# The diagonal term of a chunk's product, folded into the decay matrix by GpSimd

## The chip, the cores and the metric

The kernel runs on one core of a Trainium2 chip. The core has TensorE (matrix products, with its own queue of weight loads), VectorE, ScalarE and GpSimd (element by element), and SyncE, which here issues all DMAs. Each engine runs its own instructions in order and they wait for each other by semaphores. TensorE writes only to PSUM, and GpSimd reads only SBUF. The metric is the device time of one execution in microseconds, lower is better.

## The reference, cut to what matters

Four sequences of 512 tokens of width 256 go through a mixture of experts, a state space layer ("attention") and the mixture again. The change is in the state space layer. It has 64 heads with 128 state rows and 8 channels each, and does for each token t of each head:

```python
h  = at[..., None, None] * h + einsum('bh,bhn,bhp->bhnp', bt, B_prev, x_prev) \
                             + einsum('bh,bhn,bhp->bhnp', gt, Bt, xt)
yt = einsum('bhn,bhnp->bhp', Ct, h)
# alpha = exp(dt * A);  beta = (1 - lam) * dt * alpha;  gamma = lam * dt
```

So the state takes the token's own contribution with the weight gamma, and one step later the same contribution again with beta of the next step. All contributions of a token to later tokens have the weight `coef` = gamma + (1 - lam_next) * dt_next, times the decay; its contribution to its own output has gamma alone. That is the diagonal term.

## The kernel before, in words

An execution is two passes of three stages: the mixture for two sequences, the state space layer for each of the two, the mixture again. For the state space layer the 64 heads form 32 pairs, and the 512 tokens form 8 chunks of 64. A pair's work is spread over several turns of a software pipeline. Turn j (`turn_pe`, `turn_act`, `turn_pool`, `turn_dve`, `turn_sp`, one for each engine) treats pairs of different age side by side: projections for pair n+3 (`A`, matrix products at L61), angles for pair n+1 (`T`, L786 to L795), scaling and rotation of pair n (`F`), the chunk products of pair n-1 (`K`) and the output of pair n-2 (`Y`). Four turns (j = 0 to 3) form an iteration; one batch has 32 turns. The order within a turn is written out by hand for each engine, and nothing reorders it except that weight loads run ahead on TensorE.

The steps that matter here, in a turn:

- `F_dve1` (L885) multiplies the projections by the norm. `F_dve2` makes the decay matrix `dk` of pair n by a scan over the shift mask and the decay factors (L891), strictly below the diagonal, and a small masked copy `xwp` (L896). `F_dve3` (L909, four instructions of 128x1024) prepares the rotation, and `F_pool` (L917, L918, four of 128x512 on GpSimd) finishes it.
- `K1_pe` (L943) forms the products C·B of each chunk of pair n-1 into PSUM and transposes the rotated B (L951). `K_dve1` multiplies the products by the decay matrix into `m1` (L967) and by the diagonal mask into `m2` (L968), each in two halves of 128x256. `K2_pe` (L983) forms the chunks' states, `K_dve2` (L990, L994) runs the scan over the chunks.
- `Y1_pe` (L1005) multiplies `m1` by `x1p` and `m2` by `x2p`, 16 products of 64 tokens by 16 columns, each issued as two instructions. `x1` is x times `coef` and `x2` is x times gamma; both are made once for a batch in `prep_dve` (L720, L721), and `XP_act` (L930) puts each pair's part in place with four activations. `Y2_pe` (L1014) adds what comes from earlier chunks. Every fourth turn `Y_dve` (L1026, L1030) takes y out of PSUM.
- `ss_pe` (L827) sums squares for the norm; its second half waits for the first L846 of VectorE's turn. The second L846 of the turn waits for ScalarE's L840, which waits for the second projection (L61) of TensorE's turn.

VectorE's order in an ordinary turn is L786, L789, L846, L885 (two), L891, L896, L795, L846, L967/L968 (four), L856 in every second turn, L909 (two), L990, L994, L909 (two). TensorE's is `T` (L61), L1005, L61, L827, L1014, L61, L943 with L951, L61, L983, L61.

Of the kernel before, what the change touches and what calls it, by code (L numbers as in the profile page):

```python
# [14 lines left out]
P = 128  # L15
# [50 lines left out]
def build(nc, x_in, w_ffn, w_router, w_att, w_x, w_z, w_dtl, w_dth, a_log, w_out, bias_in, norm_w_in,  # L66
          sel_ffn_in, ident_in, cst_in, out):
    with ExitStack() as ctx:
# [67 lines left out]
        btr = sb("btr", [P, 2, SEQ])  # L136
        x1, x2 = sb("x1", [P, NH, TT, HP]), sb("x2", [P, NH, TT, HP])
        x1p = [sb(f"x1p{i}", [P, P]) for i in range(4)]
        x2p = [sb(f"x2p{i}", [P, P]) for i in range(4)]
        xwp = [sb(f"xwp{i}", [P, P]) for i in range(2)]  # L140
# [19 lines left out]
        dks = [xc[:, i, :] for i in range(2)]  # L160
        m1, m2 = sq[:, 0, :], sq[:, 1, :]
        one, cum = sb("one", [P, 1]), sb("cum", [P, SEQ])
# [498 lines left out]

        PREP_STEPS = 10
        e_pd, e_pu, e_p6 = ev("e_pd"), ev("e_pu"), ev("e_p6")
# [7 lines left out]
        def prep_dve(e, b):  # L671
# [41 lines left out]
            step(e.tensor_tensor(dlt, oml, dtk[:, 1], ALU.mult))  # L713
            step(e.tensor_tensor(coef, gam, dlt, ALU.add))
            assert n[0] == PREP_STEPS
            wide = lambda a, t: a[:, t, :].unsqueeze(2).to_broadcast([P, NH, HP])
            for t in range(TT):
                e.wait_ge(e_p2.sem, e_p2.at(TT * b + t + 1))
                src = xbanks[t][:, :].rearrange("p (n d) -> p n d", n=NH)
                e.tensor_tensor(x1[:, :, t, :], src, wide(coef, t), ALU.mult)  # L720
                ins = e.tensor_tensor(x2[:, :, t, :], src, wide(gam, t), ALU.mult)  # L721
            ins.then_inc(e_x12.sem, 1)
# [190 lines left out]
        def F_pool(e, n, j, types):  # L913
# [5 lines left out]
            if ty == 1:  # L919
                ins.then_inc(e_R.sem, 1)  # L920

        def XP_act(e, n, j, q):

            e.wait_ge(e_Y.sem, e_Y.at(n - 3))
            for dst, src in ((x1p, x1), (x2p, x2)):
                v = src[:, bass.ds(2 * q, 2) if not isinstance(q, int) else slice(2 * q, 2 * q + 2), :, :]
# [33 lines left out]
        def K_dve1(e, p, j):  # L960
            e.wait_ge(e_G.sem, e_G.at(p + 1))
            e.wait_ge(e_D.sem, e_D.at(p + 1))
            e.wait_ge(e_Y.sem, e_Y.at(p))
            half, dk = slice(0, SEQ // 2), dks[j % 2]
            for a in range(2):
                g, c = W[3 if a == 0 else 0][:, half], slice(a * SEQ // 2, (a + 1) * SEQ // 2)
                e.tensor_tensor(m1[:, c], g, dk[:, c], ALU.mult)  # L967
                ins = e.tensor_tensor(m2[:, c], g, constant("diag_mask")[:, c], ALU.mult)  # L968
            ins.then_inc(e_M.sem, 1)
# [26 lines left out]
        def Y1_pe(e, p, j, yev):  # L996
# [4 lines left out]
            for a in range(2):  # L1001
                for t in range(TT):
                    o = y[0:CL, 2 * t:2 * t + 2, PW * j + HP * a:PW * j + HP * a + HP]
                    for n, (m, x) in enumerate(((m1, x1p), (m2, x2p))):
                        e.matmul(o, m[:, (a * TT + t) * CL:(a * TT + t + 1) * CL], c4(x[j][:, :])[:, a * TT + t],  # L1005
                                 start=n == 0, stop=n == 1)

# [92 lines left out]
        def turn_pool(e, b, it, first, last):  # L1100

            N, Q, NB = b * NP + it * UN, it * UN, NP // UN
            for j in range(UN):
                n, q, p, jp = N + j, Q + j, N + j - 1, (j - 1) % UN
                T, A, SS, RG, K = in_turn(j, first, last)
                gm = b * (NP // 2) + it * 2 + j // 2
                F_pool(e, n, j, [0])
                F_pool(e, n, j, [1])
# [104 lines left out]
        def pairs_pool(e, b):  # L1213
            N, NB, G = b * NP, NP // UN, b * (NP // 2)
            turn_pool(e, b, 0, True, False)
            with e.Fori(1, NB - 1) as it:
# [269 lines left out]
```

## Time and profile before

| | us |
|---|---|
| median of 3 runs | 4703.65 |
| lowest and highest | 4689.84 and 4712.97 |
| the profiled execution | 4701.72 |
| its span | 4699.9 |
| TensorE busy in the span | 4481.7 (95%) |
| VectorE busy | 3160.8 (67%) |
| ScalarE busy | 2074.3 (44%) |
| GpSimd busy | 1383.5 (29%) |

The profile comes from one execution. In its rows PE is TensorE, PEld its weight loads, DVE VectorE, ACT ScalarE, POOL GpSimd and SP SyncE. PEclk is the granted clock of TensorE as a share of 2.4 GHz, a mean of moments at 2.4 and at 1.2 GHz. Matrix products overlap in the pipeline, so a single product's recorded time is longer than its share of the engine; the distance from one start to the next is the better measure. Busy shares are means over stages with different limits, so a stage has to be read for itself. The state space layer's pair loops lie at about 570 to 1170, 1245 to 1850, 2910 to 3510 and 3590 to 4195 us of the span.

### The profile page before, as it was taken

To read this page: it belongs to the slowest core of one execution; us is meant where nothing else is said; L and a number is where in the kernel's file an instruction comes from. 1 tells how busy PE (TensorE), PEld (TensorE's weight loads), DVE (VectorE), ACT (ScalarE), POOL (GpSimd) and SP (SyncE) were. 2 spreads that over 40 slices of the span, in tenths; PEclk is the share of its full clock that TensorE was granted. 3 is DMA by queue.
4 is the path that set the end of the run, shared out by engine and by line. 5 is a ranking of instruction groups with operands and counts; after the bars stand their busy time and mean duration, and the time that the engine had idled before them with its cause. 6 is when DMAs were issued, how large, how long until landed. Compare 5 with 4: busy or idle time off the path is not lost.

```text
span 4699.9 us, 89732 instructions
## 1 busy us (share of the span) xinstructions
PE 4481.7 (95%) x31616; PEld 3417.3 (73%) x31616; DVE 3160.8 (67%) x4157; ACT 2074.3 (44%) x3624; POOL 1383.5 (29%) x843
## 2 busy tenths in 40 slices
PE   8999899999799998999999997999988999999999
PEld 6777577877587786777667775877865787776776
DVE  5555499996599996444455554999955899954444
ACT  3333455552456552333233334555625565523332
POOL 3555133332133332111135551333321333311111
PEclk9999899997799997999999998999978999969999
DMA  4444444441444541111035544444414445411110
GB/s 151 175 175 165 155 137 147 137 142 43 131 136 141 148 128 42 57 41 41 23 142 184 186 165 140 140 148 140 134 41 134 141 134 150 124 41 47 49 44 20
DMA packets 231554, 542.73 MB, mean 115 GB/s; under 512 B 45112, under 2 KB 96320, under 8 KB 223168
## 3 DMA queue, kind: packets, MB, share of 16 engines
q1 hardware_dynamic: 231360, 540.26, 35.9%
q8 instruction: 108, 1.77, 0.2%
q14 instruction: 86, 0.70, 0.0%
HBM read 448.67 MB, written 90.44 MB: 115 GB/s over the span
## 4 chain that ended last, share of the span: by engine, by line
PE 76%; DVE 13%; issue 6%; DMA 2%; SPq 1%; ACT 1%; DVEq 1%; ACTq 0%
PE bank L61 47%; PE bank L943 4%; PE bank L983 4%; PE bank L1014 4%; PE bank L410 3%; PE bank L1005 3%; PE bank L827 3%; DVE rot L909 3%; PE bank L951 2%; DVE tmp L909 2%; DVE xbc L885 2%; DVE sqs L846 1%; PE bank L1255 1%; DVE bank L786 1%; DVE xc L891 1%
## 5 line engine op out<-in xcount | busy, mean ns | idle before, releaser
L917 POOL TENSOR_TENSOR rot<-rot,tmp 128x512 f32<-128x512 f32 x256 | 333.6, 1303 | 1918.5 <-DVE tmp L909 1918.5
L493 POOL TENSOR_TENSOR w_lo<-w_raw,w_hi 128x768 fp32r<-128x768 f32 x192 | 366.5, 1911 | 1336.5 <-ACT w_hi L453 1160.1
L61 PE MATMUL bank<-xh,wb 128*128 128x512 f32 x2048 | 704.8, 425 | 29.2 <-DVE sqs L846 26.3
L835 ACT ACTIVATE xbc<-bank,norm_w 128x512 f32<-128x512 f32 x512 | 350.3, 684 | 707.4 <-PE bank L61 699.6
L444 ACT ACTIVATE h_hi<-hf 128x512 fp32r<-128x512 f32 x384 | 242.8, 632 | 945.9 <-DVE hf L531 931.8
L526 DVE TENSOR_TENSOR h<-sg,bank 128x512 f32<-128x512 f32 x384 | 262.8, 684 | 548.1 <-PE bank L61 548.1
L61 PE MATMUL bank<-xh,w_hi 128*128 128x512 f32 x1536 | 603.7, 393 | 7.8 <-DVE xl L255 5.6
L61 PE MATMUL bank<-xl,w_hi 128*128 128x512 f32 x1536 | 600.8, 391 | 0.0
L61 PE MATMUL bank<-xh,w_lo 128*128 128x512 f32 x1536 | 597.2, 389 | 0.0
L533 DVE TENSOR_TENSOR h_lo<-hf,h_hi 128x512 fp32r<-128x512 f32 x384 | 379.0, 987 | 309.6 <-ACT h_hi L444 309.6
L61 PEld LDWEIGHTS bank<-xh,wb 128*128 128x128 f32 x2048 | 356.8, 193 | 104.8 <-DVE sqs L846 33.3
L918 POOL TENSOR_TENSOR rot<-rot,tmp 128x512 f32<-128x512 f32 x256 | 413.1, 1614 | 0.0
L909 DVE SCALAR_TENSOR_TENSOR tmp<-xbc,bias,cs_sn 128x1024 f32<-128x1024 f32 x256 | 411.9, 1609 | 0.0
L61 PE MATMUL bank<-xl,wb 128*128 128x512 f32 x1024 | 411.5, 402 | 0.0
L909 DVE SCALAR_TENSOR_TENSOR rot<-xbc,bias,cs_sn 128x1024 f32<-128x1024 f32 x256 | 359.7, 1405 | 1.5 <-PE bank L1014 1.4
L429 ACT ACTIVATE sg<-bank 128x512 f32<-128x512 f32 x384 | 229.9, 599 | 282.9 <-PE bank L61 282.0
L61 PE MATMUL bank<-h_hi,w_hi 128*128 128x512 f32 x784 | 351.8, 449 | 0.0
L61 PEld LDWEIGHTS bank<-xh,w_hi 128*128 128x128 f32 x1536 | 288.8, 188 | 69.4 <-issue 6.0
L61 PEld LDWEIGHTS bank<-xl,w_hi 128*128 128x128 f32 x1536 | 288.6, 188 | 64.9
L61 PEld LDWEIGHTS bank<-xh,w_lo 128*128 128x128 f32 x1536 | 288.7, 188 | 63.6
L885 DVE TENSOR_TENSOR xbc<-xbc,rr_bc 128x1024 f32<-128x1024 f32 x256 | 318.2, 1282 | 10.3 <-DMA rr_bc<-rr_dram 9.8
L61 PE MATMUL bank<-h_lo,w_hi 128*128 128x512 f32 x784 | 310.2, 396 | 0.0
(165 smaller groups left out, 8440.4 us busy)
## 6 DMA issues: line engine op xcount, KB each, us to landing
wb<-watt_dram SPq DMA_DIRECT2D x128, 1024.0 KB, 6.6
w_raw<-w_ffn SPq DMA_DIRECT2D x64, 1152.0 KB, 5.2
rr_bc<-rr_dram SPq DMA_DIRECT2D x128, 512.0 KB, 6.5
pw_raw<-w_att SPq DMA_DIRECT2D x64, 640.0 KB, 6.0
watt_dram<-pw_hi SPq DMA_DIRECT2D x64, 640.0 KB, 2.9
watt_dram<-pw_raw SPq DMA_DIRECT2D x64, 640.0 KB, 4.5
th<-watt_dram SPq DMA_DIRECT2D x128, 256.0 KB, 4.2
dt_bc<-row_dram SPq DMA_DIRECT2D x256, 128.0 KB, 3.1
```

The lines of the kernel that those rows point to most:

```text
L61: ins = e.matmul(dst, a, m, start=start and c == 0, stop=stop and c == n - 1, skip_group_check=not (start and stop))
L429: e.activation(sg[s][:, :], gate_bank[s][:, :], ACT.Silu).then_inc(e_silu.sem, 1)
L444: e.activation(h_hi[hslot(i, s)][:, :], hf[s][:, :], ACT.Copy).then_inc(e_hh.sem, 1)
L493: e.tensor_tensor(piece(w_lo[s], i), piece(w_raw[s], i), piece(w_hi[s], i).bitcast(F32), ALU.subtract).then_inc(e_wP.sem, 1)
L526: e.tensor_tensor(h1[s][:, :], sg[s][:, :], up_bank[s][:, :], ALU.mult).then_inc(e_h1.sem, 1)
L533: e.tensor_tensor(h_lo[hslot(i, s)][:, :], hf[s][:, :], h_hi[hslot(i, s)][:, :].bitcast(F32), ALU.subtract).then_inc(e_hl.sem, 1)
L835: e.activation(xbc[j % 4][:, i, :], XBANK[i % 2][:, :], ACT.Copy, scale=norm_w[:, i:i + 1])
L885: e.tensor_tensor(both, both, r.unsqueeze(1).to_broadcast([P, 2, SEQ]), ALU.mult).then_inc(dst.sem, 1)
L909: ins = e.scalar_tensor_tensor(o[:, 2 * ty:2 * ty + 2, :], X[:, i, :].unsqueeze(1).to_broadcast([P, 2, SEQ]), bias_of(i), cs_sn[j % 2][:, ...
L917: e.tensor_tensor(R[:, 2 * ty, :], R[:, 2 * ty, :], tmp[:, 2 * ty + 1, :], ALU.subtract)
L918: ins = e.tensor_tensor(R[:, 2 * ty + 1, :], R[:, 2 * ty + 1, :], tmp[:, 2 * ty, :], ALU.add)
L943: ins = e.matmul(o, R[h, eo, CL * k:CL * k + CL], R[h, 2 + eo, CL * k:CL * k + CL], start=eo == 0, stop=eo == 1)
```

## The change

The diagonal term is put into the decay matrix. The decay matrix has zeros on its diagonal, and `x1` carries the weight `coef`. If the diagonal gets the ratio `rho` = gamma / coef, one product with `x1` gives both terms.

- `prep_dve` makes `rho` once for a batch: a maximum with 1e-30, a reciprocal and a product on 128x256. `x2` is no longer made.
- A new step `D_pool` stands at the head of each turn on GpSimd. It multiplies the diagonal mask by the pair's eight ratios (each over 64 columns) into `own`, 128x512, and then adds `own` to the decay matrix. The sum waits for the product and for `xwp` (L896 of the kernel before), so that `xwp` is made from the matrix without its diagonal.
- `K_dve1` waits for this sum and no longer makes `m2`. `Y1_pe` has 8 products instead of 16, `XP_act` two activations instead of four.
- GpSimd waits for `x1` and `rho` before its first turn.

```order
L916 ISA
L917 TENSOR_TENSOR rot1<-rot1,tmp 128x512
L918 TENSOR_TENSOR rot1<-rot1,tmp 128x512
L916 REGISTER_ALU
L917 TENSOR_TENSOR rot1<-rot1,tmp 128x512
L918 TENSOR_TENSOR rot1<-rot1,tmp 128x512
```

And in the changed one, with line numbers that are two higher for the rotation, L931 the product and L934 the sum:

```order
L931 ISA
L931 TENSOR_TENSOR sq<-cst,rho 128x512
L932 REGISTER_ALU
L934 TENSOR_TENSOR xc<-xc,sq 128x512
L918 ISA
L919 TENSOR_TENSOR rot1<-rot1,tmp 128x512
L920 TENSOR_TENSOR rot1<-rot1,tmp 128x512
L918 REGISTER_ALU
L919 TENSOR_TENSOR rot1<-rot1,tmp 128x512
L920 TENSOR_TENSOR rot1<-rot1,tmp 128x512
```

The product follows directly upon the last rotation step of the turn before.

```diff
-        x1, x2 = sb("x1", [P, NH, TT, HP]), sb("x2", [P, NH, TT, HP])
+        x1 = sb("x1", [P, NH, TT, HP])
+        rho, cinv = sb("rho", [P, NH, TT]), sb("cinv", [P, TT, NH])
...
-        m1, m2 = sq[:, 0, :], sq[:, 1, :]
+        m1, own = sq[:, 0, :], sq[:, 1, :]
...
+            step(e.tensor_scalar(cinv[:, :, :], coef, 1e-30, None, ALU.max))
+            step(e.reciprocal(cinv[:, :, :], cinv[:, :, :]))
+            e.tensor_tensor(rho[:, :, :].rearrange("p n t -> p t n"), cinv[:, :, :], gam, ALU.mult)
...
-                e.tensor_tensor(x1[:, :, t, :], src, wide(coef, t), ALU.mult)
-                ins = e.tensor_tensor(x2[:, :, t, :], src, wide(gam, t), ALU.mult)
+                ins = e.tensor_tensor(x1[:, :, t, :], src, wide(coef, t), ALU.mult)
...
+        def D_pool(e, n, j, q):
+            blocks = lambda a: a.rearrange("p (c w) -> p c w", w=CL)
+            r = rho[:, bass.ds(2 * q, 2) if not isinstance(q, int) else slice(2 * q, 2 * q + 2), :].rearrange("p a t -> p (a t)")
+            e.wait_ge(e_Dp.sem, e_Dp.at(n))
+            e.nop(nofuse=True)
+            e.tensor_tensor(blocks(own), blocks(constant("diag_mask")), r.unsqueeze(2).to_broadcast([P, 2 * TT, CL]), ALU.mult).then_inc(e_own.sem, 1)
+            e.wait_ge(e_own.sem, e_own.at(n + 1))
+            e.wait_ge(e_xw.sem, e_xw.at(n + 1))
+            e.tensor_tensor(dks[j % 2], dks[j % 2], own, ALU.add).then_inc(e_Dp.sem, 1)
...
-            for dst, src in ((x1p, x1), (x2p, x2)):
+            for dst, src in ((x1p, x1),):
...
-            e.wait_ge(e_D.sem, e_D.at(p + 1))
+            e.wait_ge(e_Dp.sem, e_Dp.at(p + 1))
...
-                e.tensor_tensor(m1[:, c], g, dk[:, c], ALU.mult)
-                ins = e.tensor_tensor(m2[:, c], g, constant("diag_mask")[:, c], ALU.mult)
+                ins = e.tensor_tensor(m1[:, c], g, dk[:, c], ALU.mult)
...
-                    for n, (m, x) in enumerate(((m1, x1p), (m2, x2p))):
-                        e.matmul(o, m[:, (a * TT + t) * CL:(a * TT + t + 1) * CL], c4(x[j][:, :])[:, a * TT + t],
-                                 start=n == 0, stop=n == 1)
+                    e.matmul(o, m1[:, (a * TT + t) * CL:(a * TT + t + 1) * CL], c4(x1p[j][:, :])[:, a * TT + t],
+                             start=True, stop=True)
...
+                D_pool(e, n, j, q)
                 F_pool(e, n, j, [0])
                 F_pool(e, n, j, [1])
...
         def pairs_pool(e, b):
             N, NB, G = b * NP, NP // UN, b * (NP // 2)
+            e.wait_ge(e_x12.sem, e_x12.at(b + 1))
+            e.nop(nofuse=True)
```

## Rows read from the trace of the kernel before

**Rows 1.** Stretch: busy us (count) of PE, PEld, DVE, ACT, POOL; clock; DMA.

```profile
1285.00:1765.00 480.00, 476.91 (x4912) 383.06 (x4911) 438.20 (x546) 282.03 (x529) 155.91 (x109) 1.00 0.47 139
```

**Rows 2.** L786 by its line: first and last start, in two stretches.

```profile
L786 DVE SCALAR_TENSOR_TENSOR bank<-bank,dt_bc x5: 684/685/687, 1409.3 to 1480.3; 128x512 f32<-128x512 f32 x5
L786 DVE SCALAR_TENSOR_TENSOR bank<-bank,dt_bc x2: 684/684/685, 1409.3 to 1427.4; 128x512 f32<-128x512 f32 x2
```

**Rows 3.** Chain of waits through an ordinary turn: start us, us, what.

```profile
1443.40 1.97 PE bank L1005 x32
...
1446.96 1.72 PE bank L827 x4
...
1452.02 1.93 PE bank L943 x63
...
1456.39 1.69 PE bank L983 x16
...
1460.98 1.97 PE bank L1005 x32
```

**Rows 4.** VectorE's timeline, same turn: start us, us, engine, line [idle before <-releaser].

```profile
1453.37 0.69 DVE L846 TENSOR_TENSOR sqs<-bank,sqt 128x512 f32<-128x512 f32 x1 [1.37 <-ACT bank L840]
...
1454.34 0.41 DVE L968 TENSOR_TENSOR sq<-bank,cst 128x256 f32<-128x256 f32 x1
1454.67 0.41 DVE L967 TENSOR_TENSOR sq<-bank,xc 128x256 f32<-128x256 f32 x1
...
1458.12 0.40 DVE L990 TENSOR_TENSOR bank<-bank,cst 128x224 f32<-128x224 f32 x1
...
1460.35 2.29 DVE L909 SCALAR_TENSOR_TENSOR tmp<-xbc,bias,cs_sn 128x1024 f32<-128x1024 f32 x1
...
1464.51 0.67 DVE L846 TENSOR_TENSOR sqs<-bank,sqt 128x512 f32<-128x512 f32 x1
```

**Rows 5.** Reciprocals by line (min/median/max ns), and VectorE after the preparation.

```profile
L247 DVE RECIPROCAL rstd<-std x12: 177/178/179, 20.5 to 4214.8; 128x4 f32<-128x4 f32 x12
L856 DVE RECIPROCAL rc<-rc_in x64: 339/342/354, 565.1 to 4122.6; 128x32 f32<-128x32 f32 x64
1237.53 0.69 DVE L846 TENSOR_TENSOR sqs<-bank,sqt 128x512 f32<-128x512 f32 x1 [2.00 <-ACT bank L840]
```

**Rows 6.** GpSimd and VectorE side by side, and L885 by its line.

```profile
1424.16 2.25 POOL L918 TENSOR_TENSOR rot<-rot,tmp 128x512 f32<-128x512 f32 x1
...
1428.83 1.27 POOL L918 TENSOR_TENSOR rot<-rot,tmp 128x512 f32<-128x512 f32 x1
...
1425.21 2.28 DVE L909 SCALAR_TENSOR_TENSOR tmp<-xbc,bias,cs_sn 128x1024 f32<-128x1024 f32 x1
...
1429.85 1.33 DVE L885 TENSOR_TENSOR xbc<-xbc,rr_bc 128x1024 f32<-128x1024 f32 x1
L885 DVE TENSOR_TENSOR xbc<-xbc,rr_bc x256: 1198/1220/2325, 575.2 to 4146.6; 128x1024 f32<-128x1024 f32 x128
```

**Rows 7.** Waits ahead of L827 (us, times, longest) and around the one at 3667.

```profile
PE bank L827 <- DVE sqs L846: 2.7, 7, 0.9
PE bank L827 <- DVE sqs L846: 3.1, 7, 1.3
PE bank L827 <- DVE sqs L846: 3.3, 8, 1.0
...
3667.55 1.12 PE L827 MATMUL bank<-sqs,cst 128*128 128x512 f32 x2 [0.59 <-DVE sqs L846]
...
3666.00:3676.00 10.00, 9.41 (x109) 6.69 (x108) 7.09 (x10) 3.87 (x9) 1.54 (x2) 0.83 0.70 224
L786 DVE SCALAR_TENSOR_TENSOR bank<-bank,dt_bc x2: 683/684/684, 3664.9 to 3684.1; 128x512 f32<-128x512 f32 x2
```

**Rows 8.** Chain of waits at the end of a batch.

```profile
1815.78 3.21 PE bank L1005 x29
...
1834.53 1.79 PE bank L1005 x29
```

More of the change, by code:

```diff
@@ L136, in build @@
         btr = sb("btr", [P, 2, SEQ])
-        x1, x2 = sb("x1", [P, NH, TT, HP]), sb("x2", [P, NH, TT, HP])
+        x1 = sb("x1", [P, NH, TT, HP])
+        rho, cinv = sb("rho", [P, NH, TT]), sb("cinv", [P, TT, NH])
         x1p = [sb(f"x1p{i}", [P, P]) for i in range(4)]
-        x2p = [sb(f"x2p{i}", [P, P]) for i in range(4)]
         xwp = [sb(f"xwp{i}", [P, P]) for i in range(2)]
@@ L660, in prep_act @@
             e.activation(decay_t[CL:P, :, :, :], src, ACT.Copy).then_inc(e_p3.sem, 1)
-        PREP_STEPS = 10
+        PREP_STEPS = 12
         e_pd, e_pu, e_p6 = ev("e_pd"), ev("e_pu"), ev("e_p6")
@@ L920, in F_pool @@
                 ins.then_inc(e_R.sem, 1)
+        e_own, e_Dp = ev("e_own"), ev("e_Dp")
+        def D_pool(e, n, j, q):
[7 more added lines that the diff above has]
+            e.tensor_tensor(dks[j % 2], dks[j % 2], own, ALU.add).then_inc(e_Dp.sem, 1)
         def XP_act(e, n, j, q):
             e.wait_ge(e_Y.sem, e_Y.at(n - 3))
-            for dst, src in ((x1p, x1), (x2p, x2)):
+            for dst, src in ((x1p, x1),):
                 v = src[:, bass.ds(2 * q, 2) if not isinstance(q, int) else slice(2 * q, 2 * q + 2), :, :]
```

## The prediction

> **What bounds the kernel now.** I read three views: the page's busy times, then the chain of waits through one ordinary turn, then the instructions of the VectorE in the same turn. The page's busy shares, TensorE 95% and VectorE 67% of the span, are means over two kinds of stage. Inside the turns of the pair loop TensorE is busy 477 of 480 us and VectorE 438 of 480 [rows 1], so both are near their limit there, and the change touches nothing outside the attention part. The 28 turns of a batch that follow its first few repeat in rounds of four: from 1409.3 to 1480.3 us, 71.0 us [rows 2].
>
> In an ordinary turn the chain never leaves TensorE [rows 3]. From 1443.40 to 1460.98 it goes through the chunk products with x (L1005, 1.97 us), projections (L61), the row sums (L827), the products with the state (L1014), K1 (L943 and the transposes), and K2 (L983). That makes 17.58 us, and TensorE's own work fills them. VectorE is the runner-up: it stands idle 1.37 us ahead of the second L846 and hardly at L990 [rows 4]. The turn that also takes out y (L1026, L1030, every fourth) takes 18.13 us, from 1409.28 to 1427.41 [rows 2]; VectorE has no such idle time there, and TensorE waits 0.3 us for it. VectorE bounds that turn.
>
> **TensorE, removed.** Each turn loses half of L1005, 16 of 32 instructions: 1.97 / 2 = 0.98, less the lead-in that stays, about 0.93 us a turn [rows 3].
>
> **VectorE, removed and added.** Two L968 go. Each takes 0.33 us from its start to the next one's (1454.34 to 1454.67), so 0.66 us a turn [rows 4]. Before the turns, four L721 go, of the shape of L846, which is recorded at 0.69 [rows 5] (some 0.6 from start to start, 2.4 us), and three operations on 128x256 come: a maximum and a product (at 0.3 and 0.4 us) and a reciprocal. The reciprocals of the trace take 0.177 us for 4 columns and 0.342 for 32 [rows 5], 5.9 ns a column, so 256 columns are worth 1.7 us. The sum is within 0.2 us of nothing, four times in all, and VectorE afterwards stands idle 2.0 us [rows 5]. I count zero; uncovered it would be 1 us in all.
>
> **ScalarE, removed.** Two of four activations a turn, 0.48 us from start to start. ScalarE is busy 282 of 480 us [rows 1], and what waits for it waits for TensorE first. Zero.
>
> **GpSimd, added.** Each turn gets a product (mask by ratio, into `own`) and a sum (into the decay matrix), 128x512. GpSimd's operations of this shape start 1.25 us apart and it rests over 10 us a turn, so its own time costs nothing. The sum waits for L896 and its result is needed by L967 one turn later; 15 us of cover. Behind the waiting sum on GpSimd stands only L917 of the same turn, released by VectorE some 6 us later. The cost is in SBUF. Where a GpSimd operation and a VectorE operation that reads two SBUF tensors meet, one stands still: at 1424.16 GpSimd takes 2.25 instead of 1.27 us and right after it VectorE 2.28 instead of 1.27 [rows 6]. So one meeting costs 1.0 us of VectorE. The slowest L885 of the trace (2.33 instead of 1.22 us) prices it at 1.1 for just the instruction in question [rows 6].
>
> The Trainium skill ("SBUF — State Buffer", section Who interferes with whom) calls this an exclusive lock held for the whole instruction, by which the loser would stand for the full 1.25 us. The rows show 1.0 instead, so GpSimd's recorded time seems longer than its hold. By the rule the forecast would be some 7 us later; by the row it stays.
>
> Do the new ones meet anything? The product stands in GpSimd's queue right behind the last L918 and waits for nothing that is late. L918 started at 1428.83, so the product is ready at 1430.07; VectorE began L885 at 1429.85 [rows 6], and with the second L885, L891 and L896 it reads two SBUF tensors without a break for over 4 us. The product therefore always pushes in, most likely between the two L885: +1.03 us. The sum starts behind L896, while VectorE is at L795, L846 and L967, which read one operand from PSUM, and is through before L909, some 1.9 us behind L896's end. Zero, in the last turns of a batch up to 1 us, under cover there.
>
> **The sum for a round.**
> - The turn with y: VectorE bound, 18.13 + 1.03 - 0.66 = 18.50 us, 0.37 longer.
> - Two ordinary turns: the 1.03 falls into the idle 1.37 ahead of L846. TensorE's own work is 17.57 - 0.93 = 16.64. There is a loop beside it that does not hold L1005: on TensorE from the second half of L827 to the end of K2 (1446.96 + 0.86 to 1456.39 + 1.69, so 10.3 us) [rows 3], then on VectorE from L990 to the end of the L846 for which the next L827 waits (1458.12 to 1464.51 + 0.67, 7.1 us) [rows 4]. Before, the loop is 17.4. This leg holds the 1.0 us for which L909 waits at GpSimd [rows 4]. GpSimd's two now start 0.66 us earlier, since L968 is gone, while L990 stays tied to K2, so L909 meets only the end of the second: about 0.3 to 0.4 us instead of 1.0. The loop becomes 16.6 to 16.8, level with TensorE. I take 16.64: 0.93 less each.
> - The turn with a reciprocal (L856): GpSimd starts 0.26 us later and L909 meets more of it, 16.85 instead of 17.7: 0.87 less.
>
> Together 0.37 - 0.93 - 0.93 - 0.87 = -2.4 us a round.
>
> **TensorE's clock.** Behind the turn with y TensorE will now wait for L846, at L827, about 1.3 us a round instead of 0.3. At that place the trace has one wait of 0.59 us after which the granted clock fell from 2.4 to 1.2 GHz for a moment: the stretch shows 0.83 [rows 7]. The turn behind it took 19.2 us (3664.9 to 3684.1) [rows 7], 1.5 more than its fellows. But the longest waits in the same place in the three other batches, 0.9, 1.3 and 1.0 us, passed at full clock (the 1.3 stands in a stretch of 480 us with 1.00 granted) [rows 1, 7]. So between never and every round; I take one in four, 0.4 us a round, which leaves 2.0.
>
> **The ends of a batch.** In the last turns the chain is TensorE again, at the lower clock for part of it: L1005 takes 3.2 and 1.8 us [rows 8], and two more of its kind stand ahead of them; half of the four is 5 us. Some of it will turn into waits; I take 4 us a batch. The first three turns wait for DMAs and the VectorE; zero.
>
> **The sum.** 28 rounds (7 in each of 4 batches) x 2.0 = 56, and 4 x 4 = 16: 72 us. The profiled execution took 4701.7 (span 4699.9), 2 us below the median 4703.65. 4703.65 - 72 = 4632 us, 1.5% less.
>
> **Rivals.**
> 1. *No collision price*: the product slips in at no cost, and the turn with y falls by L968's 0.66 instead of growing by 0.37: -2.4 - 1.0 = -3.4 a round, x 28 = 95, and 16 more from the ends would be -111; with the clock's share, -100: 4604. For it: TensorE is the page's bound. Against it: rows 6.
> 2. *The clock falls in each round*: with 1.5 us each time, 2.4 - 1.5 = 0.9 x 28 and 16 from the ends: 4662. If it stays low twice as long, 3.0 us, the round is 0.6 longer than before and the ends pay that back: 4704. For it: the wait comes in every round. Against it: three of four such waits did nothing.
> 3. *The gain goes into the loop without L1005*: if L909 still loses 1.0 us at GpSimd, ordinary turns need 17.3, the round 70.4: -0.6 x 28 - 16 = -33: 4671. For it: the loop is 0.15 us below the period now. Against it: the shift of GpSimd by 0.66 us is plain from the order.
> 4. *Slower*: GpSimd's product reads an operand with step 0 (one ratio for 64 columns), a form that no GpSimd row here has. If it holds SBUF twice as long, each turn's VectorE loses 1.1 us more: the turn with y 19.5, ordinary ones 17.4 to 17.7 (only part is covered), the round 72.0: +1.0 x 28 = 28, with the clock's 0.4 x 28 = 11, less 16 for the ends: 4727. It decides from a hold of 1.8 us on. Against it: VectorE's L885 reads such an operand at no extra time [rows 6]. The same price if the sum meets L909 in each turn.
>
> That the work isn't removed can be excluded: half of L1005 is out of the program.
>
> **Chances.** Forecast 0.52, rival 1 0.12, rival 2 0.16, rival 3 0.12, rival 4 0.08. The range 4602 to 4690 takes in rivals 1 and 3 and the nearer half of rival 2, and leaves out rival 4. Half a per cent (24 us) is about what this kernel's measurements tell from no change. Faster by more than that: forecast 0.48, rival 1 0.12, rival 3 0.11, the nearer part of rival 2 0.07, together 0.78. Within: 0.14 (most of it rival 2's far part). Slower: 0.08.
>
> **What the changed profile would show.** L1005 with 16 instructions and 1.0 us a turn in the chain; one L885 in each turn at 2.2 to 2.3 us, and GpSimd's product recorded at 2.2; its sum at 1.3; idle time ahead of the second L846 down from 1.4 to 0.1-0.4 us; L990 waiting for L983 by about 1 us in ordinary turns; L909 in the second half of a turn stretched by 0.3 to 0.6; rounds of 68.6 us at full clock; waits of 1.3 us at L827 behind each turn with y. I am wrong if the product takes over 2.5 us, if L909's 1.0 stays, if L967 ever waits for GpSimd, or if the stretch of 480 us shows a granted clock under 0.97.

## The result, and the profile after

| | us |
|---|---|
| before, median of 4 runs beside the changed kernel | 4700.62 (4689.84 to 4712.97) |
| after, median of 4 runs | 4766.23 (4752.91 to 4785.26) |
| ratio, 95% interval | 1.0145 (1.0121 to 1.0170) |
| span of the profiled execution, before and after | 4699.9 and 4783.5 |
| granted clock over the whole span, before and after | 0.95 and 0.92 |

The change makes the kernel 1.4% slower. 4632 us was predicted, with 4602 to 4690 as the range, so the sign was wrong. The profiled execution of the changed kernel is its slowest, 19 us above the median. The slower executions are those with the lower granted clock: 4785.26 us at 0.923 and 4777.17 at 0.927, against 4755.28 at 0.933 and 4752.91 at 0.931.

First the pair loop of each of the four batches, in the busy time of the engines by stretch. The columns are those of [rows 1].

```profile
620.00:1085.00 465.00, 448.22 (x4251) 351.72 (x4244) 413.28 (x467) 259.07 (x451) 221.40 (x154) 0.97 0.46 136
1285.00:1765.00 480.00, 457.76 (x4253) 359.10 (x4252) 421.05 (x472) 260.44 (x454) 230.39 (x156) 0.94 0.46 137
2945.00:3430.00 485.00, 454.95 (x4070) 353.45 (x4069) 412.29 (x470) 263.28 (x458) 214.53 (x149) 0.94 0.47 138
3625.00:4110.00 485.00, 452.99 (x3924) 349.23 (x3923) 403.87 (x469) 267.48 (x463) 206.72 (x142) 0.93 0.44 133
```

In the stretch of [rows 1] TensorE is now busy 458 instead of 477 us, and 0.94 was granted instead of 1.00. At 1.2 or 2.4 GHz and nothing between, 0.94 means the lower level in 12% of the time. A granted clock under 0.97 in this stretch was one of the prediction's signs of being wrong. Below stands the chain of waits, the same lines in two turns: in the first turn the clock is low at L61, in the second it is full.

```profile
1427.56 1.74 PE bank L1026 x28
1429.29 2.82 PE bank L61 x6
1432.11 2.22 PE bank L957 x63
...
1464.37 1.74 PE bank L1026 x28
1466.10 1.59 PE bank L61 x6
1467.69 1.94 PE bank L957 x63
```

And the place in TensorE's own timeline where the first of these falls begins, with the granted clock around it:

```profile
1424.18 1.02 PE L829 MATMUL bank<-sqs,cst 128*128 128x512 f32 x2
1426.43 1.12 PE L829 MATMUL bank<-sqs,cst 128*128 128x512 f32 x2 [1.23 <-DVE sqs L848]
1427.48 1.80 PE L1026 MATMUL bank<-st,rot 128*64 128x16 f32 x28
1429.22 1.19 PE L61 MATMUL bank<-xh,wb 128*128 128x512 f32 x2
```

```profile
1406.00:1424.00 18.00, 17.94 (x172) 14.10 (x172) 16.50 (x19) 11.63 (x19) 9.27 (x7) 1.00 0.46 144
1424.00:1432.00 8.00, 6.77 (x40) 4.12 (x38) 7.45 (x8) 2.23 (x5) 5.25 (x4) 0.83 0.71 223
```

TensorE waits 1.23 us at L829 (L827 before), is busy again, and 2.8 us behind the wait's end a pair of L61 takes 1.19 us where such a pair takes 0.62 to 0.74 at full clock.

Next, VectorE's timeline (start, us, engine, line, idle time before it) in the turn that has the reciprocal and follows an ordinary one, with GpSimd's and SyncE's beside it. It answers to [rows 4] and [rows 6].

```profile
1405.73 0.69 DVE L788 SCALAR_TENSOR_TENSOR bank<-bank,dt_bc 128x512 f32<-128x512 f32 x1
...
1408.17 3.32 DVE L887 TENSOR_TENSOR xbc<-xbc,rr_bc 128x1024 f32<-128x1024 f32 x2
1411.41 1.21 DVE L893 TENSOR_TENSOR_SCAN xc<-cst,al_bc 128x512 f32<-128x512 f32 x1
...
1416.38 0.35 DVE L858 RECIPROCAL rc<-rc_in 128x32 f32<-128x32 f32 x1 [0.88 <-DMA rc_in<-decay_t]
...
1423.76 0.69 DVE L788 SCALAR_TENSOR_TENSOR bank<-bank,dt_bc 128x512 f32<-128x512 f32 x1
```

```profile
1407.14 1.28 POOL L920 TENSOR_TENSOR rot<-rot,tmp 128x512 f32<-128x512 f32 x1
1408.38 2.03 POOL L931 TENSOR_TENSOR sq<-cst,rho 128x512 f32<-128x512 f32 x1
1413.15 1.28 POOL L934 TENSOR_TENSOR xc<-xc,sq 128x512 f32<-128x512 f32 x1 [2.75 <-DVE xwp L898]
```

```profile
1412.83 1.19 SPq L768 DMA_DIRECT2D al_bc<-row_dram  x2
1414.23 0.68 SPq L867 DMA_DIRECT2D rc_in<-decay_t  x1
```

The product (L931) pushes in between the two L887, as foreseen: the pair takes 3.32 us, and it takes 2.45 to 2.47 where nothing pushes in. L893, the scan, therefore starts 0.9 us later. On SyncE the load of `al_bc` waits for this scan, and the load of `rc_in` stands behind it in the same queue. It is issued at 1414.23, and the chain of waits shows it on its way until 1416.35:

```profile
1414.23 2.12 DMA rc_in<-decay_t
```

VectorE stands 0.88 us at L858 for it. This turn takes 18.03 us from L788 to L788, where 16.85 was predicted. The 28 turns of its kind take 17.85 to 18.98 us, 18.14 in the median.

An ordinary turn goes as predicted in its parts and not in its length:

```profile
1388.77 0.69 DVE L788 SCALAR_TENSOR_TENSOR bank<-bank,dt_bc 128x512 f32<-128x512 f32 x1
...
1397.16 0.69 DVE L848 TENSOR_TENSOR sqs<-bank,sqt 128x512 f32<-128x512 f32 x1 [0.56 <-ACT bank L842]
...
1401.90 0.40 DVE L1003 TENSOR_TENSOR bank<-bank,cst 128x224 f32<-128x224 f32 x1 [0.98 <-PE bank L996]
1402.33 0.69 DVE L1007 TENSOR_TENSOR_SCAN st<-end_bc,bank 128x256 f32<-128x256 f32 x1
1402.94 1.67 DVE L911 SCALAR_TENSOR_TENSOR rot<-xbc,bias,cs_sn 128x1024 f32<-128x1024 f32 x1
```

VectorE waits 0.98 us for K2, and L911 in the second half is stretched from 1.28 to 1.67, 0.4 us (0.3 to 0.6 was forecast). The idle time ahead of the second L848 is 0.56 us, where 0.1 to 0.4 was forecast. The turn takes 1405.73 - 1388.77 = 16.96 us, not 16.64. Its chain alternates now between TensorE (L829 to L996) and VectorE (L1003 to L848); L1017 isn't in it.

The waits of the stretch 1285 to 1765 (us in all, times, longest), to be held against [rows 7]:

```profile
PE bank L829 <- DVE sqs L848: 21.7, 14, 3.0
DVE bank L1003 <- PE bank L996: 16.6, 12, 3.4
DVE rc L858 <- DMA rc_in<-decay_t: 7.9, 7, 1.6
```

**Where the 83.6 us of the profiled executions are.** I took the starts of L786 (L788) in the 28 turns of each batch that repeat, 112 turns in all, and the trace's clock records, and added up. A turn "at full clock" is the median of its kind over the turns that hold no moment at the low clock.

| | before | after |
|---|---|---|
| a round at full clock: turn with y, ordinary, with reciprocal, ordinary | 18.14 + 17.56 + 17.58 + 17.72 = 71.00 | 18.34 + 16.96 + 18.14 + 17.04 = 70.48 |
| 112 turns | 1992.9 | 2067.1 |
| of them at the low clock | 17 | 232 |
| ends of the four batches | 363.9 | 369.0 |
| first turns of the four batches | 327.2 | 325.7 |
| the rest | 2015.8 | 2021.8 |

"First turns" is the stretch from the stage's first subtraction of the mean (`xc`) to the first of the 28 turns, "ends" that from the last of them to the last addition to the residual (`xs`). So 28 rounds gained 28 x 0.52 = 15 us at full clock, and 74 + 15 = 89 us went with the low clock. For 215 us more at the low clock that is 0.41 us each. Ends, first turns and rest make +9.6.

### The profile page after: what moved, and what is told of

Its sections match the earlier page's. It is cut to its first block, busy times and chain, and to the rows that moved or that the text cites. A ratio compares the mean times of both kernels' runs of the same rounds, so it can differ in the third digit from the quotient of the medians.

```text
span 4783.5 us, 85810 instructions
## 1 busy us (share of the span) xinstructions
PE 4495.5 (94%) x29568; PEld 3389.6 (71%) x29568; DVE 3158.8 (66%) x3897; ACT 2022.3 (42%) x3368; POOL 1758.4 (37%) x1099
## 3 DMA queue, kind: packets, MB, share of 16 engines
q8 instruction: 102, 1.67, 0.1%
## 4 chain that ended last, share of the span: by engine, by line
PE 64%; DVE 18%; issue 10%; DMA 3%; SPq 2%; DVEq 1%; ACT 1%; ACTq 0%
PE bank L61 41%; PE bank L957 4%; DVE xbc L887 4%; DVE rot L911 4%; PE bank L410 3%; PE bank L1026 3%; PE bank L996 3%; DVE tmp L911 2%; DVE sqs L848 2%; PE bank L965 2%; PE bank L829 2%; DVE bank L788 2%; DMA rc_in<-decay_t 1%; DVE xc L893 1%; SPq L768 1%
## 5 line engine op out<-in xcount | busy, mean ns | idle before, releaser
L61 PE MATMUL bank<-xh,wb 128*128 128x512 f32 x2048 | 738.2, 443 | 26.8 <-DVE sqs L848 23.9
L919 POOL TENSOR_TENSOR rot<-rot,tmp 128x512 f32<-128x512 f32 x256 | 332.4, 1298 | 849.4 <-DVE tmp L911 849.4
L61 PE MATMUL bank<-xh,w_hi 128*128 128x512 f32 x1536 | 605.9, 394 | 6.1 <-DVE xl L255 3.9
L61 PE MATMUL bank<-xl,w_hi 128*128 128x512 f32 x1536 | 603.1, 393 | 0.0
L61 PE MATMUL bank<-xh,w_lo 128*128 128x512 f32 x1536 | 599.5, 390 | 0.0
L61 PEld LDWEIGHTS bank<-xh,wb 128*128 128x128 f32 x2048 | 375.6, 203 | 106.8 <-DVE sqs L848 30.9
L61 PE MATMUL bank<-xl,wb 128*128 128x512 f32 x1024 | 427.0, 417 | 0.0
L887 DVE TENSOR_TENSOR xbc<-xbc,rr_bc 128x1024 f32<-128x1024 f32 x256 | 414.0, 1656 | 9.2 <-DMA rr_bc<-rr_dram 9.1
L911 DVE SCALAR_TENSOR_TENSOR tmp<-xbc,bias,cs_sn 128x1024 f32<-128x1024 f32 x256 | 392.6, 1534 | 0.0
L920 POOL TENSOR_TENSOR rot<-rot,tmp 128x512 f32<-128x512 f32 x256 | 387.6, 1514 | 0.0
L829 PE MATMUL bank<-sqs,cst 128*128 128x512 f32 x512 | 274.0, 624 | 96.6 <-DVE sqs L848 93.9
L931 POOL TENSOR_TENSOR sq<-cst,rho 128x512 f32<-128x512 f32 x128 | 242.0, 1891 | 329.3 <-DVE x L723 329.3
L911 DVE SCALAR_TENSOR_TENSOR rot<-xbc,bias,cs_sn 128x1024 f32<-128x1024 f32 x256 | 358.1, 1399 | 0.1
L61 PE MATMUL bank<-h_hi,w_hi 128*128 128x512 f32 x784 | 351.6, 449 | 0.0
L61 PEld LDWEIGHTS bank<-xh,w_hi 128*128 128x128 f32 x1536 | 290.3, 189 | 68.1 <-issue 4.2
L61 PEld LDWEIGHTS bank<-xl,w_hi 128*128 128x128 f32 x1536 | 289.9, 189 | 65.4
```

Source lines behind the costliest of these rows:

```text
L61: ins = e.matmul(dst, a, m, start=start and c == 0, stop=stop and c == n - 1, skip_group_check=not (start and stop))
L829: e.matmul(SSB[:, :], one_hot[:, 6 - 2 * c:6 - 2 * c + P], sqs[:, ty, :], start=c == 0, stop=c == 3, skip_group_check=True).then_inc(e_ssm ...
L887: e.tensor_tensor(both, both, r.unsqueeze(1).to_broadcast([P, 2, SEQ]), ALU.mult).then_inc(dst.sem, 1)
L911: ins = e.scalar_tensor_tensor(o[:, 2 * ty:2 * ty + 2, :], X[:, i, :].unsqueeze(1).to_broadcast([P, 2, SEQ]), bias_of(i), cs_sn[j % 2][:, ...
L919: e.tensor_tensor(R[:, 2 * ty, :], R[:, 2 * ty, :], tmp[:, 2 * ty + 1, :], ALU.subtract)
L920: ins = e.tensor_tensor(R[:, 2 * ty + 1, :], R[:, 2 * ty + 1, :], tmp[:, 2 * ty, :], ALU.add)
```

## The experiments

Each kernel is timed against the kernel before on the same chip, and the ratio is to that: the median of the kernel before was 4705.66 us beside experiments 1 to 4, 4702.94 beside 5 to 8 and 4695.90 beside 9 to 12. Differences in us between two experiments are those of their medians. "Round" is the sum of four turns at full clock, and "low" the time at the low clock within the 112 turns, both of the profiled execution, in us.

| kernel | us | ratio to before (95%) | round | low |
|---|---|---|---|---|
| before | 4703.65 | 1 | 71.0 | 17 |
| after | 4766.23 | 1.0145 (1.0121 to 1.0170) | 70.5 | 232 |
| 1: without GpSimd's two | 4660.88 | 0.9913 (0.9879 to 0.9947) | 69.0 | 75 |
| 2: before, with GpSimd's two | 4758.73 | 1.0103 (1.0078 to 1.0127) | 72.4 | 31 |
| 3: product behind L898 | 4667.95 | 0.9918 (0.9894 to 0.9941) | 69.1 | 65 |
| 4: TensorE filled in two turns | 4694.91 | 0.9987 (0.9965 to 1.0008) | 70.4 | 58 |
| 5: `rc_in` ahead of `al_bc` | 4673.41 | 0.9944 (0.9928 to 0.9961) | 69.5 | 85 |
| 6: 3 and 5 | 4635.03 | 0.9864 (0.9838 to 0.9890) | 68.7 | 38 |
| 7: 3 and 4 | 4642.19 | 0.9871 (0.9844 to 0.9897) | 69.0 | 20 |
| 8: each L1017 twice | 4693.53 | 0.9978 (0.9961 to 0.9996) | 70.6 | 10 |
| 9: filled behind the turn with y | 4771.27 | 1.0144 (1.0110 to 1.0178) | 70.5 | 160 |
| 10: filled behind the reciprocal | 4730.43 | 1.0068 (1.0043 to 1.0093) | 70.5 | 188 |
| 11: before, with 5's order | 4695.92 | 0.9995 (0.9980 to 1.0011) | 71.0 | 17 |
| 12: 6, filled behind the turn with y | 4644.73 | 0.9876 (0.9846 to 0.9906) | 68.7 | 31 |

**1. Without GpSimd's two operations.** L981 waits for the scan alone, and the diagonal term is left out of the result.

```diff
-            e.wait_ge(e_Dp.sem, e_Dp.at(p + 1))
+            e.wait_ge(e_D.sem, e_D.at(p + 1))
...
-                D_pool(e, n, j, q)
```

> The changed kernel without GpSimd's product and sum (the diagonal term is left out). Theory C (clock and lateness): GpSimd's product holds L887 by 1.0 us, which lengthens the turn with y, opens a wait of TensorE at L829 in every round and so lets the granted clock fall. Without it the turn with y needs 18.13 - 0.66 = 17.5 us, the others 16.7 to 17.0, the round about 68; the granted clock in the stretches of the pair loop is back at 0.99 to 1.00; 4701 - 3 x 28 - 16 = about 4600 us, ratio 0.98. Rival P (TensorE's own loss of work is enough to let the clock fall): the clock stays at 0.93 to 0.97 and the time over 4650. Rival V (GpSimd's hold alone, clock without weight): the time falls by 1.03 x 128 = 132 us against the changed kernel, 4635.

Measured 4660.88, 0.9913 (0.9879 to 0.9947). The whole loss against before is gone and a small gain stands, so the loss comes with GpSimd's two operations. But what is left, 43 us, is far less than the 72 and more that half of L1005 and two L968 were worth in the working, and the time is not the 4600 of theory C but over 4650, as rival P has it. The round is 2.0 us shorter than before, and the low clock has 75 us where before it had 17: a part of the falls comes with what the change takes away, without GpSimd.

**2. GpSimd's two alone**, added to the kernel before; they write a scratch tile.

```diff
+            e.tensor_tensor(rho[:, :, :].rearrange("p n t -> p t n"), coef, gam, ALU.mult)
...
+                D_pool(e, n, j, q)
...
+            e.tensor_tensor(own[:, :], dks[j % 2], own[:, :], ALU.add).then_inc(e_Dp.sem, 1)
```

> The kernel before with GpSimd's product and sum added in the same places (they write a tile of their own, nothing reads it; the waits are those of the changed kernel). Theory C: the turn with y grows by 1.0 to 19.1, L858 waits 0.9 us for its DMA in every second reciprocal turn, TensorE waits at L827 by 1.3 us a round, the clock falls there in most rounds (1.5 us or more): 2 to 4 us a round, 4755 to 4815. Rival V: 1.0 us in the turn with y and nothing else, 28 us: 4729. Rival P (the fall of the clock comes from TensorE's lost products, which are all back here): granted clock 1.00 in the pair loop.

Measured 4758.73, 1.0103 (1.0078 to 1.0127). The turn with y takes 18.98 instead of 18.14 us, so the push costs 0.84 there, and the turn with the reciprocal 18.07 instead of 17.58. The second of these can't come from VectorE's slack, which was enough; it is the same turn that is too long in the changed kernel. The clock is nearly undisturbed here (31 us low), with all of TensorE's products in place. So the time lies in theory C's range, but not for its reason: it had the clock fall in most rounds, and 43 us of the 61 between the two profiled executions are in the turns, 39 of them at full clock.

**3. The product starts later**, behind L898, directly ahead of the sum.

```diff
         def D_pool(e, n, j, q):
...
+            e.wait_ge(e_xw.sem, e_xw.at(n + 1))
+            e.nop(nofuse=True)
             e.tensor_tensor(blocks(own), blocks(constant("diag_mask")), r.unsqueeze(2).to_broadcast([P, 2 * TT, CL]), ALU.mult).then_inc(e_own.sem, 1)
             e.wait_ge(e_own.sem, e_own.at(n + 1))
-            e.wait_ge(e_xw.sem, e_xw.at(n + 1))
```

> The changed kernel with GpSimd's product waiting for L898 as the sum does, so that neither meets L887 and L893. Theory C: L887 takes 1.22 us each, L893 starts 1.0 us earlier, L858 no longer waits for its DMA, the turn with y falls to 17.4 us; the sum may hold the first L911 by up to 0.6 us in ordinary turns. If the wait at L829 goes, the clock stays up: round 68 to 69, about 4630 us. Rival P: the clock falls all the same, over 4680. Rival V: 4766 less 1.03 x 28 (turns with y only) = 4737.

Measured 4667.95, 0.9918 (0.9894 to 0.9941), not to be told from experiment 1. GpSimd does the same work as in the changed kernel, so its work costs nothing that shows and its place costs 98 us. About 4630 was expected: the low clock still has 65 us. GpSimd's and VectorE's timelines of this kernel:

```profile
1419.33 1.04 POOL L933 TENSOR_TENSOR sq<-cst,rho 128x512 f32<-128x512 f32 x1 [4.00 <-DVE xwp L898]
1420.45 1.27 POOL L935 TENSOR_TENSOR xc<-xc,sq 128x512 f32<-128x512 f32 x1
```

```profile
1415.10 2.45 DVE L887 TENSOR_TENSOR xbc<-xbc,rr_bc 128x1024 f32<-128x1024 f32 x2
1417.47 1.21 DVE L893 TENSOR_TENSOR_SCAN xc<-cst,al_bc 128x512 f32<-128x512 f32 x1
...
1439.65 0.35 DVE L858 RECIPROCAL rc<-rc_in 128x32 f32<-128x32 f32 x1 [0.25 <-DMA rc_in<-decay_t]
```

The product takes 1.04 us alone and 2.03 where it meets L887, so it stood 1.0 us. From the pair's start to the start of L893 it is 3.24 us in the changed kernel and 2.37 here (1417.47 - 1415.10), so VectorE stood 0.9. Both sides of the meeting pay. The wait at L858 has shrunk from 0.88 to 0.25.

**4. Full TensorE at the waits.** Three of the six instructions of the projection ahead of L829 (L61) are issued twice, some 0.7 us, in the turns behind the one with y and behind the one with the reciprocal.

```diff
+                if again:
+                    split_matmul(e, XBANK[i % 2][:, :], [(pair_w(wb[j % 2], i, 0), xpair[0])], True, True)
...
-                    A_pe(e, n + 3, j + 3, ac, [0])
+                    A_pe(e, n + 3, j + 3, ac, [0], j % 2 == 0)
```

> The changed kernel with three of the twelve instructions of a projection product (0.7 us of 512-column work, same result) issued twice ahead of L829 in every second turn, those behind the turn with y and behind the turn with the late DMA. Theory C: TensorE has more work, but in the place of the idle time, the granted clock of the pair loop rises from 0.94 to 0.99 or more, and the kernel becomes faster than the changed one: rounds of 70.3 to 71 us, 4690 to 4710. Rival V (the clock without weight): no faster than the changed kernel, 4766 to 4805 (0.7 x 56 more at most).

Measured 4694.91, 0.9987 (0.9965 to 1.0008): 71 us less than the changed kernel, by more work on TensorE. Its turns at full clock are those of the changed kernel (18.34, 16.96, 18.06, 17.05). What differs is the clock, and the waits at L829 (L831 here):

```profile
1285.00:1765.00 480.00, 469.83 (x4516) 367.72 (x4517) 435.06 (x492) 269.32 (x473) 232.73 (x164) 0.99 0.46 138
```

```profile
PE bank L831 <- DVE sqs L850: 9.4, 15, 1.5
DVE rc L860 <- DMA rc_in<-decay_t: 6.8, 7, 1.3
```

The wait at the reciprocal is still there, 7 times; 9.4 us of waits at L831 go with a granted clock of 0.99, and 21.7 us with 0.94. (A low clock also lengthens the waits, so not all of the 12 us is cause.) Between the two traces lie 73.7 us in the 112 turns for 174 us of low clock, again 0.42 us for each.

**5. SyncE's order.** The load of `rc_in` and what belongs to it stands ahead of that of `al_bc`.

```diff
+                if RG:
+                    R_sp(e, gm + 1, (j // 2 + 1) % 2, b * NB + it + 1)
                 if not (last and j >= 2):
                     e.wait_ge(e_D.sem, e_D.at(n + 1))
                     e.nop(nofuse=True)
                     al_sp(e, q + 2, j + 2)
-                if RG:
-                    R_sp(e, gm + 1, (j // 2 + 1) % 2, b * NB + it + 1)
```

> The changed kernel with SyncE's order turned round in the two turns of a round that have a reciprocal: the DMA to the reciprocal's input (and the two behind it) ahead of al_bc, which waits for L893. Theory Q: L893 comes 1.0 us later since GpSimd's product holds L887, al_bc is issued later and the DMA behind it too, and this is why L858 stands 0.9 us in the fourth turn of a round. With the order turned the wait goes and that turn falls from 18.0 to 17.1 or 17.2; with less lateness the clock falls less often; 4766 - 0.9 x 28 = 4741 without the clock, down to 4710 with it. Rival: the DMA itself is what is late (its request or its landing), and the turn stays at 18.0, the time at 4766.

Measured 4673.41, 0.9944 (0.9928 to 0.9961): 93 us less than the changed kernel. The meeting is as it was, and L858 no longer waits. This is the turn with the reciprocal behind an ordinary one, from L788 at 1434.64 to L788 at 1451.78, 17.14 us:

```profile
1437.08 3.31 DVE L887 TENSOR_TENSOR xbc<-xbc,rr_bc 128x1024 f32<-128x1024 f32 x2
1440.31 1.21 DVE L893 TENSOR_TENSOR_SCAN xc<-cst,al_bc 128x512 f32<-128x512 f32 x1
...
1444.32 0.34 DVE L858 RECIPROCAL rc<-rc_in 128x32 f32<-128x32 f32 x1
```

The turn with the reciprocal falls from 18.14 to 17.14 us, and the low clock from 232 to 85 us. So the late DMA has a price of its own (28 x 1.00 = 28 us) and one through the clock, which is why the time is below the 4710 to 4741 expected. Of the 15 falls that are left, 12 begin behind the turn with y.

**6. Both repairs**, 3 and 5 together. The edit is the two diffs above.

> The product late (as in e3) and SyncE's order turned round. L893 is early again in e3, where L858 waited little (2.4 us in a stretch of 480). The turn of 17.4 to 17.6 us can fall to 17.1: at most 0.4 x 28 = 11 us below e3's 4668, so 4655 to 4668, same as e3 within its noise.

Measured 4635.03, 0.9864 (0.9838 to 0.9890). This is the best version of the study: faster than before by 1.4%, and faster than 3 and 5, each of which it contains, by 33 and 38 us. At most 11 was expected below 3. Of the 26 us by which its 112 turns are shorter than 3's, some 10 are in the rounds at full clock, and with the rest goes less low clock (38 us for 65). Its round at full clock is 17.57 + 16.96 + 17.14 + 17.05 = 68.7 us.

```profile
1425.40 0.34 DVE L858 RECIPROCAL rc<-rc_in 128x32 f32<-128x32 f32 x1
1428.85 0.40 DVE L1004 TENSOR_TENSOR bank<-bank,cst 128x224 f32<-128x224 f32 x1 [0.81 <-PE bank L997]
```

**7. The late product with the filling** of 4.

> The product late (as in e3) and the three projection products issued twice ahead of L829 in every second turn (as in e4). At full clock e3's round is 17.57 + 16.96 + 17.45 + 17.05 = 69.0 us, 28 of them 1933, and e3's turns took 1957: so the clock still costs it 24 us. Theory C: the fill takes most of that back, 4645 to 4655. Rival: TensorE has no more room, since its own work is 16.64 a turn and the fill makes two turns 17.3: 0.3 us more in each of 56 turns, 4668 to 4690.

Measured 4642.19, 0.9871 (0.9844 to 0.9897). 26 us less than 3 alone. With the product late the low clock is 65 us and with the filling 20.

**8. Each L1017 twice.** TensorE has its 32 instructions back; everything else is the changed kernel.

```diff
-                    e.matmul(o, m1[:, (a * TT + t) * CL:(a * TT + t + 1) * CL], c4(x1p[j][:, :])[:, a * TT + t],
-                             start=True, stop=True)
+                    for _ in range(2):
+                        e.matmul(o, m1[:, (a * TT + t) * CL:(a * TT + t + 1) * CL], c4(x1p[j][:, :])[:, a * TT + t],
+                                 start=True, stop=True)
```

> The changed kernel with each of the eight products of L1017 issued twice (same result): TensorE's work is again what it was before, but VectorE, ScalarE, GpSimd and the DMAs are those of the changed kernel. It tells whether the lost products cost anything by being lost. Theory C: they filled 0.93 us ahead of L829 with work; TensorE comes to its wait 0.93 us later and stands 0.93 us less there, and the clock falls less often: faster than the changed kernel, 4700 to 4740, although TensorE does more. At full clock the turn with y stays 18.34, the others become 17.57 at the most: 71.5. Rival: small products don't hold the clock; the time stays at 4766 or rises to 4790.

Measured 4693.53, 0.9978 (0.9961 to 0.9996): 73 us less than the changed kernel, with 0.93 us more TensorE work in each turn. The stretch of [rows 1], the chain in an ordinary turn, and the wait at L829 in the stretch:

```profile
1285.00:1765.00 480.00, 478.26 (x4932) 385.58 (x4931) 439.15 (x495) 270.46 (x475) 232.53 (x165) 1.00 0.46 139
```

```profile
1441.79 1.97 PE bank L1018 x32
...
1445.35 1.72 PE bank L829 x4
...
1454.77 1.69 PE bank L996 x16
```

```profile
PE bank L829 <- DVE sqs L848: 1.7, 2, 1.2
```

In this turn the chain never leaves TensorE, the waits at L829 are down from 21.7 to 1.7 us, and the clock is full. The round takes about as long as in the changed kernel at full clock (70.6 and 70.5): there the halved L1017 gained next to nothing, since VectorE with its late DMA is level with TensorE's full work. It opened the waits behind which the clock falls.

**9 and 10. One filling at a time**: 4 in the turn behind the one with y only (`j == 2`), or behind the one with the reciprocal only (`j == 0`).

> The fill of e4 (three projection products issued twice) only in the turn behind the turn with y. The changed kernel has two late turns in a round: that with y, in which GpSimd's product holds VectorE, and the fourth, in which L858 waits for its DMA. If the fall of the clock starts behind the turn with y, this fill takes nearly all of the 72 us that e4 won: 4695 to 4710. If it starts behind the fourth turn, 4750 to 4766. If each of the two late turns makes the falls more frequent: between.

> The fill of e4 only in the turn behind the fourth, the one with the late DMA. The mirror of e9: 4750 to 4766 if the fall starts behind the turn with y, 4695 to 4710 if it starts behind the late DMA, between if both count.

Measured 4771.27, 1.0144 (1.0110 to 1.0178), and 4730.43, 1.0068 (1.0043 to 1.0093). One filling brings nothing, the other half. The falls move to the place that isn't filled: in 9, 21 of 26 begin behind the turn with the reciprocal, in 10, 25 of 29 behind the turn with y; in the changed kernel it is 18 and 12 of 34. So each of the two waits is enough by itself, and in all three kernels there is about one fall a round behind the two together (30, 23 and 25 in 28 rounds). The two effects do not add up: 4 brings 71, 9 brings -5 and 10 brings 36.

**11. The kernel before with 5's order.**

> The kernel before with SyncE's order turned round as in e5. Theory Q: in the kernel before L858 hardly waits (it is not among the waits of the stretch of 480 us), so the order is worth nothing there: 4695 to 4710, same. Rival: the order is a gain of its own, independent of the change, and the 93 us of e5 are mostly that: 4610 to 4660.

Measured 4695.92, 0.9995 (0.9980 to 1.0011). The order of SyncE costs nothing as long as the scan is on time.

**12. Version 6 with the filling behind the turn with y.**

> The best version so far (product late, order turned round, e6 at 4635) with the fill in the turn behind the turn with y. In e6's turns the clock was low for 37 us, at 0.4 us lost for each (after against e4) some 15 us. If the fill keeps it up: 4620 to 4630. If the fill's 0.7 us cost more than they save: 4635 to 4650.

Measured 4644.73, 0.9876 (0.9846 to 0.9906). No better than 6, whose interval it overlaps; 31 us of low clock against 38 leave little to win in the turns.

## Why the prediction was wrong

The prediction gave -72 us, and the profiled executions differ by +83.6 (the medians by +65.6). The 155.6 us between them, by its own steps:

| step | predicted | measured | miss |
|---|---|---|---|
| clock, in the turns | +11 | +89 | 78 |
| 28 rounds at full clock | -67 | -15 | 52 |
| ends of a batch | -16 | +5 | 21 |
| first turns and rest | 0 | +4.5 | 4.5 |

**"The sum for a round", the turn with a reciprocal: failed.** 16.85 us was predicted and 18.14 measured, 1.29 x 28 = 36 of the 52 us. I worked out where L885 and L909 meet GpSimd, and did not follow what VectorE releases. SyncE's `al_bc` waits for L891 (L893 in the changed kernel), which the push delays, and `rc_in` is queued behind it. Experiment 5 takes the wait away and gives 17.14, experiment 2 brings it into the kernel before, and experiment 11 shows that without the push the order is harmless. The 0.3 us from 16.85 to 17.14 stand in experiments 5 and 6 alike. The wait was in the trace of before already, where it was rare. This is the turn ahead of the one fall that the prediction knew of, at 3667:

```profile
3657.65 0.35 DVE L856 RECIPROCAL rc<-rc_in 128x32 f32<-128x32 f32 x1 [0.67 <-DMA rc_in<-decay_t]
```

**"TensorE's clock": failed, the largest term.** "One in four" was drawn from three waits that had passed and one that had not [rows 7], and they were read at the wrong place. Those of 0.9, 1.0 and 0.59 us, the one with the fall among them, are not behind the turn with y but behind the one with the reciprocal, and only the one of 1.3 us is behind a turn with y. Ahead of each of the four, L856 had waited 0.67 to 0.94 us for `rc_in`. The mechanism was rival 2's, but it had 0.16, and it knew of one wait a round. In fact there are two a round, since the late DMA makes a second behind the turn with the reciprocal, and 9 and 10 show that one is enough to bring the clock down in most rounds. The loss is 3.2 us a round where 0.4 was put. The Trainium skill ("TensorE: Matmul & The Clock Gate", section A second HAM failure mode: psum-queue depth-cycling) tells that short idle times between groups of matmuls can make the clock go back and forth. This case agrees: with 14 waits at L829, 21.7 us in all, the granted clock of the stretch is 0.94, and with two, 1.7 us in all, it is 1.00 (experiment 8).

That the clock and not the filling's other effects brings the time back rests on two different fillings. 4 adds other instructions at another place than 8, both have the changed kernel's round at full clock within 0.1 us, and they end within 1.5 us of each other.

**The same step, ordinary turns: rival 3 in part.** 16.96 and 17.04 instead of 16.64, 0.7 us a round. L911's 1.67 came as forecast; the loop without L1005 was put at 16.6 to 16.8 and is 16.96. It takes the same 16.96 in experiments 1 and 3, where no push lengthens it, so it isn't the push either. I read the loop from rows with other waits in them and took the lower end.

**The turn with y: right.** 18.50 predicted, 18.34 measured. The push between the two L885 was there in 106 of the 112 turns; its price was 0.9 for 1.03. Compared with experiment 3, which has 17.57, it costs the turn 0.77 us. The product with the step-0 operand is recorded at 2.03 in the median, which rival 4 might take for its own, but alone it takes 1.04, less than the other operations of GpSimd (1.27). Rival 4's mechanism is refuted; that the kernel became slower, as it had it, is chance.

The rule of the Trainium skill on this port ("SBUF — State Buffer", section Who interferes with whom) fits better than I allowed: L887 stands still for 0.9 of the product's 1.04 us, and the product for 1.0 of the 1.22 us of an L887.

**Right:** the sum meets nothing in all but 4 of 128 turns (1.28 us in the median), L981 never waits for GpSimd, the preparation costs nothing; its reciprocal was put at 1.7 us:

```profile
L716 DVE RECIPROCAL cinv<-cinv x4: 1753/1753/1753, 552.8 to 3651.8; 128x256 f32<-128x256 f32 x4
L931 POOL TENSOR_TENSOR sq<-cst,rho x128: 1033/2028/2047, 557.7 to 4240.7; 128x512 f32<-128x512 f32 x128
```

**"The ends of a batch": failed, and open.** -16 was predicted and +5 measured. These stretches vary between 341 and 386 us over all kernels, mostly along with the time for which the clock is low there (212 us low in experiment 6 with 341.4, 314 us low in experiment 9 with 386.2), and no experiment shows what sets this. It leaves some 20 us of each difference between two kernels unexplained.

**With both repairs the sum was right in size.** Experiment 6 has a round of 68.7 us where the prediction had 68.6, and 4635 us where it had 4632. It gets there in another way, and that the totals agree is chance: the turn with y is 0.9 us shorter than I gave it and the others together 1.0 longer. Still, the saving was in the change, and was lost by where the product stands in GpSimd's queue and what stands behind `al_bc` in SyncE's.

**Open:** why one wait brings the clock down and another doesn't. Within the 112 turns of the changed kernel TensorE waits at L829 28 times behind the turn with the reciprocal, by 0.9 to 2.2 us, and 18 falls begin in these turns; behind the turn with y it waits 27 times, by 1.25 us or more, and 12 falls begin. In experiment 4 there are 56 such waits, most of them of 0.5 to 0.8 us, and 8 falls. The size of the wait goes with the falls, but among waits of one size, 1.25 to 1.3 us, some pass and some don't, and no experiment tells them apart. TensorE's busy time does not sort them either: experiment 3 has it busy 471 of 485 us at a granted clock of 0.96, and experiment 2 462 of 485 at 0.99.

The filling behind the turn with y alone (9) gives nothing in the medians, though its profiled execution has 72 us less low clock in the turns than that of the changed kernel. Its turns are 26 us shorter there and its ends 17 us longer, which leaves 10 us, and the profiled execution of the changed kernel is 19 us above its median where that of 9 is 4 above. What makes its ends longer is not shown.

## What to carry to other kernels

When an operation is delayed, follow everything that its engine releases, the DMA queue above all: a load that stands in order behind one that waits for the delayed operation is late as well, though nothing in it depends on that operation. When work is taken from a TensorE that is full, ask whether another loop is level with it; if so the gain is a row of short waits, and their price can be a lower clock that costs more than the work did. Put new GpSimd work where VectorE reads one operand from PSUM, not where it reads two from SBUF.

## What the runs showed of the hardware that I had not expected

- Issuing TensorE's products at L1017 twice made the kernel 73 us faster: the granted clock of the stretch rose from 0.94 to 1.00 with TensorE busy 478 instead of 458 of 480 us.
- A microsecond at the low clock cost 0.41 to 0.42 us of the turns, in two comparisons that share the changed kernel's trace.
- A meeting of GpSimd and VectorE at SBUF is paid on both sides: 1.0 us on the product (2.03 for 1.04) and 0.9 on the pair L887 (3.24 for 2.37 from its start to that of L893).
- GpSimd's product with a mask and a ratio that is the same for 64 columns takes 1.04 us for 128x512, and its rotation and its sum, of the same size, 1.27 to 1.28.
